# Routing's one-hot tiles, slots outside and experts inside, in a four-layer kernel on one NeuronCore

## The reference

```
scores = softmax(x @ gate_w.T)                     # 16 experts
chosen = top 4 by (score, then lower index)
weight = score / sum of the chosen four
place[token, e] = number of earlier tokens that chose e     # kept if < 128 (CAPACITY)
for e in 16:  slots[e] = tokens kept by e, in order; 
              y[token] += weight * (silu(xs @ w_gate[e]) * (xs @ w_up[e])) @ w_down[e]
y += shared expert (256 -> 352 -> 256);   q = rope(x @ Wq.T);  k, v = x @ Wk.T, x @ Wv.T
```

## Time and profile before

| | |
|---|---|
| time, median of 3 runs | 1037.59 us (1036.47 to 1038.67) |
| the profiled execution's own time | 1039.74 us |
| its span, first to last instruction | 1037.9 us |
| TensorE's mean granted clock, share of full speed | 0.984 |
| the route stage in it, first to last instruction of TensorE | 452.8 to 516.6 us |

### The profile page before, as it was taken

The page is one execution under the profiler, slowest core; times in us unless marked ns, Lnnn a source line. Parts: engine busy times, 40 slices in busy tenths (PEclk is TensorE's granted clock), DMA queues, the critical chain, the costliest instruction groups (busy, mean ns, idle before and its releaser), DMA issues. The chain is left out here.

```text
span 1037.9 us, 13747 instructions
## 1 busy us (share of the span) xinstructions
PE 978.0 (94%) x4692; PEld 601.0 (58%) x4692; DVE 692.9 (67%) x1080; ACT 488.1 (47%) x1036; POOL 285.1 (27%) x248
## 2 busy tenths in 40 slices
PE   6999989989999999999798999989999999999997
PEld 4455654466665665645555555656676676555554
DVE  2989877379999999869245555655666604567653
ACT  3632234798887886322145445536666601111112
POOL 0000020028887888210023222003554500000000
PEclk9999999999999999999889999989999999999999
DMA  4113123040000000064054443220000001101001
GB/s 129 43 66 107 41 75 112 8 117 22 21 32 20 23 11 2 1 191 142 11 145 111 100 94 70 52 62 1 1 1 2 1 1 31 61 31 30 30 1 40
DMA packets 53951, 52.84 MB, mean 51 GB/s; under 512 B 9864, under 2 KB 48872, under 8 KB 53888
## 3 DMA queue, kind: packets, MB, share of 16 engines
q1 hardware_dynamic: 48352, 46.00, 14.8%
q0 software_dynamic: 3072, 4.20, 2.4%
q10 hardware_dynamic: 2464, 1.84, 0.6%
HBM read 44.45 MB, written 5.47 MB: 48 GB/s over the span
## 5 line engine op out<-in xcount | busy, mean ns | idle before, releaser
L1106 POOL TENSOR_TENSOR seen<-state,c_row 128x512 f32<-128x512 f32 x128 | 160.6, 1276 | 100.2 <-DVE state L1126 72.9
L1126 DVE TENSOR_TENSOR_SCAN state<-decay,banks 128x512 f32<-128x512 f32 x128 | 155.3, 1216 | 14.8 <-issue 7.3
L2490 PE MATMUL banks<-xnT,weight 128*128 128x512 f32 x256 | 115.0, 592 | 1.0 <-PEq L2217 1.0
L1064 ACT ACTIVATE weighed_x<-dx_tok,b_tok 128x512 f32<-128x512 f32 x124 | 87.7, 709 | 25.7 <-PE banks L1236 24.4
L2224 POOL TENSOR_TENSOR prob<-prob,inverse 128x512 f32<-128x512 f32 x64 | 65.2, 1039 | 113.2 <-DVE inverse L2309 113.2
L1074 ACT ACTIVATE decay<-delta_pairs,A 128x510 f32<-128x510 f32 x128 | 90.5, 707 | 6.2 <-DVE state L1126 6.2
L1236 PEld LDWEIGHTS banks<-ident,weighed_x 128*128 128x128 f32 x512 | 58.6, 140 | 59.2 <-ACT weighed_x L1064 33.3
L2531 DVE TENSOR_TENSOR inter<-gelu,banks 128x512 f32<-128x512 f32 x32 | 22.0, 688 | 96.7 <-ACT gelu L2522 96.0
L2522 ACT ACTIVATE gelu<-banks 128x512 f32<-128x512 f32 x32 | 19.1, 597 | 138.2 <-PE banks L2490 138.2
L1236 PE MATMUL banks<-ident,weighed_x 128*128 128x128 f32 x512 | 80.1, 279 | 2.3 <-DVE state L1126 2.3
L2490 PEld LDWEIGHTS banks<-xnT,weight 128*128 128x128 f32 x256 | 48.6, 190 | 49.3 <-issue 47.8
(11 more groups left out here) (386 smaller groups left out, 1795.8 us busy)
## 6 DMA issues: line engine op xcount, KB each, us to landing
prob_row<-probs_dram SPq DMA_DIRECT2D x8, 512.0 KB, 3.7
c_row<-c_dram SPq DMA_DIRECT2D x32, 128.0 KB, 2.9
slot_wide_w<-in_L_ffn_w_gate SPq DMA_DIRECT2D x16, 176.0 KB, 2.5
slot_wide_w<-in_L_ffn_w_up SPq DMA_DIRECT2D x16, 176.0 KB, 2.5
slot_down_w<-in_L_ffn_w_down SPq DMA_DIRECT2D x16, 176.0 KB
gate_up_w<-in_L_ffn_gate_up_w SPq DMA_DIRECT2D x8, 256.0 KB, 2.8
delta_pairs<-conv_in SPq DMA_DIRECT2D x8, 256.0 KB, 3.5
w_WqT<-in_L_attn_W_q SPq DMA_DIRECT2D x1, 2048.0 KB, 12.5
```

What stands on the lines that cost most here:

```text
L1064: nc.scalar.activation(weighed[:, v % 2, tile, :, j, :], dx_tok[:, 4 * p + tile, :].rearrange("p (g e) -> p g e", g=groups), ACT.Identity, ...
L1106: nc.gpsimd.tensor_tensor(seen[:, u % ring, :], state[:, u % ring, :], c_row[:, v % 4, :], ALU.mult).then_inc(seen_ready, 1)
L1126: nc.vector.tensor_tensor_scan(state[:, u % ring, :], decay[:, u % ring, :, :].rearrange("p b t -> p (b t)"), banks[:, 4 + u % 2, :], 0.0, ...
L2490: last = nc.tensor.matmul(banks[:, 4 + 2 * half + j, :], weight[:, s, j, k, tile * P:(tile + 1) * P], xnT[:, k, cols[half]], start=(k == 0 ...
```

## The change

The one-hot tiles get another layout, other types in the comparison, and one tile more. `one_hot` is now [token, tile, slot, expert] instead of [token, tile, expert, slot]. A new tile `slot_rows` holds the slot number, in 16 bits, repeated for the 16 experts; GpSimd makes it once from the loaded `slots`, before it works on the query weights, and waits for `rest_weights` ahead of it. The last step on `place` writes a 16-bit tile, `place_bf`. The comparison reads `slot_rows` and `place_bf`, both of 16 bits, with experts as the innermost dimension of all three tiles. VectorE waits for `slot_rows` once. The table's products take `one_hot[:, t, :, e]` as stationary operand: 128 elements with a step of 16 elements, 32 bytes.

```diff
@@ route_stage: tiles and semaphores
-        one_hot = m.sbuf("one_hot2", [P, NT, EXPERTS2, CAPACITY], BF16)
+        one_hot = m.sbuf("one_hot2", [P, NT, CAPACITY, EXPERTS2], BF16)
+        slot_rows = m.sbuf("slot_rows2", [P, CAPACITY, EXPERTS2], BF16)
+        place_bf = m.sbuf("place_bf2", shape, BF16)
+        slot_rows_ready = nc.alloc_semaphore("slot_rows_ready2")
@@ GpSimd
                 nc.gpsimd.memset(v[:, :, HEAD2 + 1:], 0.0).then_inc(consts_ready, 1)
+                pool.wait_ge(*rest_weights)
+                nc.gpsimd.tensor_copy(slot_rows[:, :, :], w["slots"][:, :].unsqueeze(2).broadcast_to([P, CAPACITY, EXPERTS2])
+                                      ).then_inc(slot_rows_ready, 1)
                 pool.wait_ge(*query_weights_loaded)
@@ TensorE
                 for e in range(EXPERTS2):
                     for t in range(NT):
-                        last = nc.tensor.matmul(banks[:, 0, e * INFO:(e + 1) * INFO], one_hot[:, t, e, :],
+                        last = nc.tensor.matmul(banks[:, 0, e * INFO:(e + 1) * INFO], one_hot[:, t, :, e],
                                                 info[:, t, e, :], start=(t == 0), stop=(t == NT - 1))
@@ VectorE
-                steps.do(nc.vector.tensor_scalar(place[:, :, :], place[:, :, :], -1.0, None, ALU.add))
+                steps.do(nc.vector.tensor_scalar(place_bf[:, :, :], place[:, :, :], -1.0, None, ALU.add))
+                dve.wait_ge(slot_rows_ready, 1)
                 for t in range(NT):
                     ins = nc.vector.tensor_tensor(
-                        one_hot[:, t, :, :], w["slots"][:, :].unsqueeze(1).broadcast_to([P, EXPERTS2, CAPACITY]),
-                        place[:, t, :].unsqueeze(2).broadcast_to([P, EXPERTS2, CAPACITY]), ALU.is_equal)
+                        one_hot[:, t, :, :], slot_rows[:, :, :],
+                        place_bf[:, t, :].unsqueeze(1).broadcast_to([P, CAPACITY, EXPERTS2]), ALU.is_equal)
```

## The result

The changed kernel takes 1055.6 us (median of 4 runs, 1054.33 to 1057.3) against 1037.23 us: a ratio of 1.0176, 95% interval 1.0156 to 1.0197, some 18 us slower. The difference of the medians is 18.4 us, of the two profiled spans 17.6. The profiled execution took 1057.3 us over a span of 1055.5, against a span of 1037.9 before.

The account below looks back on a forecast made before the run. TensorE is busy nine tenths or more, so time is lost where it waits; 14.4 + 3.0 - 2.1 + 2.6 = 17.9 us on a median of 1037.6 gives 1055.5 us, range 1047 to 1063.5.

Parts of the forecast that it names:

- (1): Ahead of the query weights: GpSimd waits for the rest loads until 461.5, then copies for 2.2 us; with (2) +14.4 us.
- (2): Query weights: GpSimd and VectorE alternate on SBUF operands, so the first query product starts at 474.3, not 459.88; with (1) +14.4 us.
- (3): Query products after the stall: six microseconds at half clock do the work of three, +3.0 us.
- (4): One-hot tiles before the table: 16-bit comparisons take 1.22 us; only the last two tiles count, -2.1 us.
- (5): The table's 128 products: the 32-byte step in the stationary operand costs 20 ns more each, +2.6 us.
- (6): Clock after the shorter wait at the stage's end: falls in the table, the down product runs as before, 0 us.
- Turns: Start of the stage: GpSimd and VectorE alternate on SBUF operands, delaying the query weights; part of the +14.4 us stall.
- Not slower: Rival: early release of GpSimd, query stall of 4.8 us, clock holds, free loads; sum -0.3, 1037.3 us; chance 0.03.
- no turns: Rival at the query weights: the engines do not hold each other, stall 7.7 us, sum 11.2, 1048.8 us; chance 0.15.
- dear loads: Rival at the table: strided stationary loads at 127 ns a product, 1065.7 us; chance 0.17.
- free loads: Rival at the table: the strided stationary operand costs nothing, 1052.9 us; chance 0.12.
- a clock that holds at the end: Rival at the stage's end: after a 3.8 us wait the down product saves 3.0 us at full clock, 1052.5; chance 0.13.

Follow-up runs that it names:

- e1: The changed kernel with GpSimd's wait and copy into slot_rows moved behind the three instructions on the query weights; ratio 1.0022 to the kernel before.
- e2: The kernel before plus the wait and copy ahead of the query weights and VectorE's wait for it, slot_rows unread; ratio 1.0131.
- e3: The kernel before plus only the wait for the rest loads ahead of the query weights, no copy; one run, queries 11.1 us late.
- e5: The changed kernel with VectorE held before rank_mask until the query weights are done; one run, queries 5.3 us sooner than in the changed kernel.
- e7: The changed kernel with 13 idle TensorE products ahead of the wait for the query weights; table 4.25 us sooner than in the changed kernel.
- e4: The kernel before with only the changed one_hot layout, comparison still of 32-bit operands; ratio 1.0046, table 8.04 us.
- experiment 9: g2 with two one-hot tiles ahead of each of the first four shared halves; 1028.35 us against 1038.86 for the kernel before, ratio 0.9896.
- g2: e1 with experts in groups of 2, a 4-byte step in the table's stationary operand; one run, 1037.44 us beside 1039.34 for the kernel before.
- g8: e1 with experts in groups of 8, a 16-byte step in the table's stationary operand; one run, 1041.73 us beside 1039.34 for the kernel before.
- e10: The kernel before, its own layout, with both comparison operands in 16 bits; one run, 1037.05 us beside 1038.86 for the kernel before.

## Why the prediction was right

The time, 1055.6, is the predicted 1055.5 to a tenth. That close it is luck: the terms are off by up to 1.9 us, two were not foreseen, and they cancel. The mechanism of the large terms, a stall made by a wait and stretched by turns, with half clock behind it, is shown by e1, e2, e3, e5 and e7.

| term | predicted | measured in the profile |
|---|---|---|
| (1), (2) stall of the queries | +14.4 | +13.05 |
| (3) half clock in the queries | +3.0 | +2.76 |
| clock at the shared products | not foreseen | +1.62 |
| (4) last one-hot tiles | -2.1 | -2.14 |
| (5) the table's products | +2.6 | +4.48 |
| (6) down product | 0 | -1.32 |
| start of the next stage | not foreseen | -2.36 |
| the rest, nearly all in the fourth layer | 0 | +1.5 |
| sum | +17.9 | +17.6 |

*Turns*: right, by e3 and e5. The stall is 1.3 us shorter than the sum: L204 ended 0.28 us sooner, the copy held 1.75 us and not 2.2, L205 and L207 2.14 and not 2.29 each, and the first two instructions on the weights 1.13 and not 1.26.

*The clock*: that it falls on a wait of this kind and is dear for some five microseconds was right, and e7 takes the price away. The idle time before the fall was taken too long: the window at 0.86 in the earlier trace rows puts it at 498.72, 5.0 us after the last product, and in the stall it came at 464.66, 4.6 us after. So the stall of 4.8 us in the rival "Not slower" was no sure case of a clock that holds. That it also fell behind the values' narrow products was missed.

*The one-hot tiles*: right to 0.04 us. Only the two tiles behind the last shared half count, and six faster ones turned into idle time of VectorE.

*The table*: mis-sized, by 1.9 us. The step "I take the difference, 20 ns" took a row with two 32-bit elements to a 16-byte line as the price for one with none beside it; it is 35 ns. The upper bound, a lost fast load, was far off. The estimate of 3.5 us that stands beside the Trainium skill's page SBUF — State Buffer, section SBUF "cachelines", was nearer than my term.

*The end*: "the down product runs as before" was wrong by 1.3 us. The clock fell in the longer table, sooner against the down product's start, and was back after 3 of its microseconds in place of 6. The start of the next stage, at half clock before from 519 to 526 us, was at full clock: -2.36 us. Both come from when the clock falls and returns, and in e1, with the same table of 8.04 us, neither came: its down product took 13.76 us, and the next stage began at half clock again. The missed +1.62 and these -3.7 cancel the table's error. The rest of +1.5 us comes in the first products of the fourth layer, far behind the change: the delay is 16.1 us from the attention stage to the end of the third layer and 17.6 some 30 us later and to the end. Among its parts, the 32 products of L2121 (L2128 now) took 3.67 us in place of 5.36, TensorE's idle time behind the transposes was 3.31 in place of 1.75, and the eight of L2159 (L2166) 6.50 in place of 3.67, at half clock. Code and data there are the same, and the runs of the changed kernel alone lie 3.0 us apart.

*The rivals*: no turns is out by e3 and e5, dear loads at 127 ns by 62, free loads by e4, a clock that holds at the end by the window from 516. The release that "not slower" needed did not come: the wait ended at 461.98.

## What to carry to other kernels

Ahead of an instruction that another engine waits for, do not put a wait for something else, however small the work behind it: here one line cost 11 us, the copy 2. Before GpSimd's work is moved, look at what VectorE does with two SBUF operands at that time, and count each instruction as one turn. If a layout is changed for one engine's pace, keep two to four elements within 16 bytes for the engine that reads it with a step; and if tiles get faster, change the order too, or all but those at the end turn into idle time.

## What the runs showed of the hardware

GpSimd and VectorE took turns, one whole instruction each, wherever these rows show both at work on SBUF and VectorE with two operands, GpSimd's one-operand copy too: a product of GpSimd takes 1.26 us alone (e5) and 3.30 with a VectorE instruction between. A reduction of one operand (L208) overlapped GpSimd's L1439 and neither was longer.

The price of a step in a 16-bit stationary operand of 128 x 128 with six moving columns: 27, 27, 33, 60 and 62 ns a product at 2, 4, 8, 16 and 32 bytes.

The clock fell in stretches where TensorE showed as busy. In the changed kernel it fell about 1 us into the table of 6-column products, behind a wait of 3.76 us; in experiment 9 the same kind of table without a wait kept it. Behind the router's 32 products of 16 columns, with no idle time above 0.5 us, it fell in seven of the fourteen profiled executions (the keys or the router's own products at half clock) and stayed in the other seven. So in kernels that differ nowhere before it, the first query product came 7.08, 8.78 (g2, g8) or 10.41 us (e10) into the stage, for the clock alone: differences of up to some 3 us between single executions of this kernel are not an edit's.
